# Attention loop of a fused Macaron layer on eight cores: V's projection issued in half pieces, and one more eviction on ScalarE

## The chip, the cores and the metric

The program runs on all 8 cores of one Trainium2 chip. Each core computes one of the 8 sequences of the batch by itself; nothing is exchanged between cores. The metric is the device time of the slowest core in microseconds (us). Everything is in fp32.

## The reference, cut to what matters

```
x = x + 0.5 * ffn(layernorm(x))        # 32 experts x 4 sets, argmax over groups of 32 tokens
x = x + attn(layernorm(x))             # 16 heads of 64, learned relative positions
x = x + 0.5 * ffn(layernorm(x))

def attn(x):                           # x: [2048, 1024] for one core
    Q, K, V = x @ Wq.T + bq, x @ Wk.T + bk, x @ Wv.T + bv      # 16 heads x 64
    scores = (Q K^T + Q . rel_table[clip(i - j + 1023, 0, 2046)]) / 8
    out = softmax(scores) V
    return out @ Wo.T + bo
```

## The kernel before

The kernel is one straight program for each engine, written out by Python loops. An engine runs its own instructions in the order in which they were written; a wait is on a semaphore that another engine raises. What `do(...)` returns is such a token, and `wt(engine, token, ...)` makes the engine wait for it before its next instruction.

**Stages.** The first feed-forward part, then its combine, which also computes the layer norm, transposes it into `HBASE` and projects Q, K and V for the first pair of heads; then the attention loop; then the second feed-forward part with its combine. The change touches the attention loop and the part of the first combine that issues projections.

**The attention loop** (in `emit_attn`) goes over 8 pairs of heads `p`, and for each pair over 16 blocks `q` of 128 query rows: 128 blocks `n = 16 p + q`. A block has four quarters `c` = 0 to 3. In a quarter TensorE gets, in this order:

1. `emit_t(.., 0)`: half of the transposes of 512 columns of the block before (first half, 8 small transposes). They are written to the PSUM banks at `BK_T`, of which there is one set, so they wait for `t_free`, the eviction of the quarter before.
2. `emit_content`: Q K^T for 512 keys (banks `BK_C`).
3. `emit_qr`: Q times the position table for block `n + 2` (banks `BK_Q`), for as many chunks as the block has, 3 or 4. It waits for `qr_free`, the ScalarE eviction of the chunk before.
4. in quarter 2 `emit_rz`, a small transpose.
5. `emit_t(.., 1)`: the second half of the transposes; then `evict_t` copies all 1024 columns to SBUF. Which engine does so depends on the group `g` of transposes: VectorE for `g` 0 and 3, ScalarE for 1 and 2. Group `g` is evicted in quarter `(g + 1) % 4`, so groups 3, 0, 1 and 2 belong to quarters 0, 1, 2 and 3.
6. pieces of the next pair's projections from a `queue` (below).
7. `emit_pv`: probabilities times V for the group of the quarter before.

VectorE adds the two score parts (L888) and takes the maximum (L898) in each quarter. ScalarE evicts the position chunk (L802, L808), and at the end of quarter 3 `emit_softmax` gives it two Exp instructions of 128 x 2048 (L919). In `emit_attn` all this stands in the program ahead of the quarter's pieces.

**The queue of pieces.** `pieces_k`, `pieces_v` and `pieces_q` yield functions. A K or Q projection of 512 tokens is 4 pieces of 2 matmuls, and after the fourth ScalarE evicts it (L689). A V projection of 128 tokens is one piece of 8 matmuls with an eviction on VectorE (L706). All of them share one PSUM bank in the loop, `BK_PJ` (in the combine there are two, `BK_PV` too):

```
pj["banks"] = [BK_PJ]
if part == 0:
    wt("tensor", wtok, pj[bank], h_tok[4 * nb + 2], h_tok[4 * nb + 3])
```

`pj[bank]` is the token of the last eviction from the bank. For pairs 1 to 6 the queue is: the 4 last pieces of Q of this pair, 16 of K, 16 of V, 12 of Q (three quarters of it) of the next pair, 48 in all; for pair 0 it is 44, for pair 7 only 4. Within a pair they are spread over the 64 quarters by this rule:

```
target = max(-(-len(queue) * (4 * q + c + 1) // 64),
             min(len(queue), 4 * q + c + 1, 4))
while done < target:
    queue[done]()
    done += 1
```

In what follows a quarter is written block.quarter, as 13.3 for block 13 of a pair, quarter 3.

Of the kernel before, what the change touches and what calls it, by code (L numbers as in the profile page):

```python
# [15 lines left out]
NPAIR = 8  # L16
NT = 16
# [42 lines left out]
def build_nc():  # L60
# [5 lines left out]
    wvt = nc.dram_tensor("wvt", [DM, DM], F32, kind="ExternalInput").ap()  # L66
# [22 lines left out]
    with ExitStack() as stack:  # L89
# [39 lines left out]
        def ap(off, dims, p0=0, np_=128):  # L129
            return AP(SCR[:, :].tensor, p0 * SCRW + off, [[SCRW, np_]] + dims)  # L130
# [6 lines left out]
        def wt(eng, *toks):  # L137
            for t in toks:
                if t is not None:
                    b.wait(eng, t[0], t[1])  # L140
# [3 lines left out]
        def do(eng, fn, sig=True):  # L144
            if not sig:
                b.op(eng, fn)
                return None
            return (SEM[eng], b.op(eng, fn, inc=SEM[eng]))

        def dma(eng, out, in_, sem):  # L150
            return (sem, b.dma(eng, out, in_, sem))

        def mm(out, lhsT, rhs, start, stop, sig=False, tr=False):
            if tr:
                return do("tensor", lambda e: e.matmul(  # L155
                    out, lhsT, rhs, start=start, stop=stop,
                    is_transpose=True), sig)
            return do("tensor", lambda e: e.matmul(  # L158
                out, lhsT, rhs, start=start, stop=stop), sig)
# [470 lines left out]
        def emit_attn(ffn, in_hbm, src_hbm):  # L630
# [3 lines left out]
            WQ, WK, WV = 6144, 46208, 47232  # L634
# [17 lines left out]
            def load_w(src, off, p, sem):  # L652
                return dma("sync", ap(off, [[128, 8], [1, 128]]),
                           AP(src.tensor, 128 * p,
                              [[DM, 128], [128 * DM, 8], [1, 128]]), sem)
# [11 lines left out]
            h_tok = {}  # L667

            pj = {"banks": [BK_PJ, BK_PV], "i": 0, BK_PJ: None, BK_PV: None}
            state = {"q": [None] * 4, "k": [None, None],  # L670
                     "v": [None, None], "wk": w_k, "wv": w_v, "wq": w_q}
# [19 lines left out]
                    AF.Identity, bias=scr(bof + p, bof + p + 1), scale=scale))  # L691
                return tok

            def proj_v_piece(p, c):
                pj["i"] += 1
                bank = pj["banks"][pj["i"] % len(pj["banks"])]
                wt("tensor", state["wv"] if c == 0 else None, pj[bank],
                   h_tok[c])
                tok = None
                for m in range(8):  # L700
                    tok = mm(PS[:, bank:bank + 128],
                             ap(HBASE + 2048 * m + 128 * c, [[1, 128]]),
                             ap(WV + 128 * m, [[1, 128]]),
                             m == 0, m == 7, sig=(m == 7))
                wt("vector", tok)
                pj[bank] = state["pj"] = do("vector", lambda e: e.tensor_tensor(  # L706
                    ap(VT[p % 2] + 128 * c, [[1, 128]]),
                    PS[:, bank:bank + 128],
                    ap(BVR + 128 * p, [[1, 128]]), ALU.add))
                return tok  # L710

            def pieces_k(p):
                for nb in range(4):
                    for part in range(4):
                        def piece(nb=nb, part=part):
                            tok = proj_qk_piece(p, KT[p % 2], WK, BK, 1.0,
                                                state["wk"], nb, part)
                            if tok:
                                state["k"][p % 2] = state["pj"]
                            if tok and nb == 3 and p + 1 < NPAIR:  # L720
                                wt("sync", tok)
                                state["wk"] = load_w(wkt, WK, p + 1, "wka")
                        yield piece

            def pieces_v(p):
                for c in range(NT):
                    def piece(c=c):
                        tok = proj_v_piece(p, c)
                        state["v"][p % 2] = state["pj"]
                        if c == NT - 1 and p + 1 < NPAIR:  # L730
                            wt("sync", tok)
                            state["wv"] = load_w(wvt, WV, p + 1, "wva")
                    yield piece

            def pieces_q(p, nbs):
                for nb in nbs:
                    for part in range(4):
                        def piece(nb=nb, part=part):
                            tok = proj_qk_piece(p, QT, WQ, BQS, 0.125, state["wq"],
                                                nb, part)  # L740
                            if tok:
                                state["q"][nb] = state["pj"]
                            if tok and nb == 3 and p + 1 < NPAIR:
                                wt("sync", tok)
                                state["wq"] = load_w(wqt, WQ, p + 1, "wqa")
                        yield piece
# [225 lines left out]
            def evict_t(n, g):  # L972
                tok = t_done[n]
                slot = g % 2
                eng = "vector" if g in (0, 3) else "scalar"
                wt(eng, tok, pt_free[slot])
                if eng == "vector":
                    t_free[0] = do("vector", lambda e: e.tensor_copy(  # L978
                        ap(PT[slot], [[1, 1024]]), PS[:, BK_T:BK_T + 1024]))
                else:  # L980
                    t_free[0] = do("scalar", lambda e: e.activation(  # L981
                        ap(PT[slot], [[1, 1024]]), PS[:, BK_T:BK_T + 1024],
                        AF.Copy, scale=1.0))
                pt_tok[(n, g)] = t_free[0]
# [3 lines left out]
            def emit_pv(n, g):  # L988
# [15 lines left out]
                if g == 3:  # L1004
# [12 lines left out]
                    if q % 4 == 3 and n < LAST:  # L1017
# [11 lines left out]
            todo = []  # L1029
            pk, pq, pv = (list(pieces_k(0)), list(pieces_q(0, range(4))),  # L1030
                          list(pieces_v(0)))

            def emit_h_tr(t):
                k = next_pair()
                wt("tensor", hx_t[t], pair_free[k])
                for m in range(8):
                    tok = mm(PS[:, 1024 * k + 128 * m:1024 * k + 128 * (m + 1)],
                             ap(HX[t % 2] + 128 * m, [[1, 128]]),
                             IDENT[:, :], True, True, sig=(m == 7), tr=True)
                tr_t[t] = tok  # L1040
                wt("scalar", tok)
                h_tok[t] = do("scalar", lambda e: e.activation(
                    ap(HBASE + 128 * t, [[2048, 8], [1, 128]]),
                    PS[:, 1024 * k:1024 * (k + 1)], AF.Copy, scale=1.0))
                pair_free[k] = h_tok[t]
                if t % 4 == 3:
                    nb = t // 4
                    todo.extend(pk[4 * nb:4 * nb + 4] + pq[4 * nb:4 * nb + 4]
                                + pv[4 * nb:4 * nb + 4])
                if t == 3:  # L1050
                    todo.extend(lambda n=n, ci=ci: emit_qr(n, ci, True)()
                                for n in (0, 1) for ci in range(4))

            def per_tile(t, src, y):
                if t >= 1:
                    emit_h_tr(t - 1)
                hx_t[t] = emit_ln_tile(t, src, HX[t % 2], y,
                                       (tr_t.get(t - 2),))
                for _ in range(4):
                    if todo:  # L1060
                        todo.pop(0)()
                return (hx_t[t],)
# [37 lines left out]
            for n in range(NIT):  # L1100
                p, q = n // 16, n % 16
                if q == 0:
                    queue = []
                    if p > 0:
                        queue += pieces_q(p, (3,))
                    if p + 1 < NPAIR:
                        queue += pieces_k(p + 1)
                        queue += pieces_v(p + 1)
                        queue += pieces_q(p + 1, range(3))
                    done = 0  # L1110
                for c in range(4):
# [10 lines left out]
                    if tr >= 0:  # L1122
                        emit_t(tr // 4, tr % 4, 1)
                        evict_t(tr // 4, tr % 4)
# [18 lines left out]
            emit_t(NIT - 2, 3, 0)  # L1143
            emit_t(NIT - 2, 3, 1)
            evict_t(NIT - 2, 3)
            emit_pv(NIT - 2, 2)
            emit_pv(NIT - 2, 3)
# [90 lines left out]
```

How the kernel before makes its waits and increments, by code:

```python
    def wait(self, eng, semname, val):  # L40
        if val is None or val <= 0:
            return
        s = self.sems[semname]
        self.th[eng].append(lambda e, s=s, v=val: e.wait_ge(s, v))
# [1 line left out]
    def op(self, eng, fn, inc=None, n=1):  # L46
        if inc is None:
            self.th[eng].append(fn)
            return None
        self.cnt[inc] += n
        s = self.sems[inc]
        self.th[eng].append(lambda e, fn=fn, s=s, n=n: fn(e).then_inc(s, n))
        return self.cnt[inc]
```

## Time and profile before

| | |
|---|---|
| median of 3 runs | 3952.4 us (3952.1 to 3977.1) |
| the profiled execution, its own time | 3966.1 us |
| span of its slowest core (core 1) | 3964.1 us |
| spans of the 8 cores | 3927.9 to 3964.1 us |
| mean granted TensorE clock of the cores | 0.938 to 0.946 |
| attention loop in the span | about 685 to 3215 us |

The profile is of one execution; the rows below are of its slowest core. Start times count from the first instruction of the span. TensorE is PE, VectorE is DVE, ScalarE is ACT, and PEld is the weight load beside the matmuls. A matmul in fp32 shows as two instructions, so a piece of 2 matmuls is 4 of them and 8 matmuls are 16.

### The profile page before, as it was taken

How to read it: one execution, taken by the hardware profiler on the slowest of the kernel's cores; microseconds unless marked ns; L12 is line 12 of the kernel's file. 1: busy time of each engine (PE TensorE's matmuls, PEld its weight loads, DVE VectorE, ACT ScalarE, POOL GpSimd, SP SyncE). 2: the span in 40 equal slices, each digit the busy share in tenths (PEclk: the TensorE clock that was granted, in tenths of full speed). 3: DMA queues.
4: the chain of work that ended last, by engine and by line, in shares of the span. 5: the costliest groups of instructions: out<-in, count | busy, mean ns of one | idle time of the engine just before them, and what ended most of it. 6: DMA issues, size and time to landing. Idle time of an engine off the chain costs nothing.

```text
span 3964.1 us, 80834 instructions; the slowest of 8 cores (3927.9 to 3964.1 us)
## 1 busy us (share of the span) xinstructions
PE 3500.4 (88%) x29664; PEld 2215.0 (56%) x29664; DVE 2097.3 (53%) x2703; ACT 1561.0 (39%) x2013; POOL 187.9 (5%) x289
## 2 busy tenths in 40 slices
PE   6988469999999999999999999999987789988842
PEld 4776134565566566566557557556654545567610
DVE  4333223666666666666666666666675733333311
ACT  3222122544554554554454454455454411122200
POOL 0000000000000000000000000000000000000001
PEclk8799687999999999999999999999998989999965
DMA  4557883564565565465466456456468711156697
GB/s 135 170 188 248 308 257 118 180 200 162 171 208 171 165 206 178 158 203 189 157 193 197 150 184 208 156 173 212 153 188 248 222 55 64 59 178 211 222 320 264
DMA packets 248833, 736.25 MB, mean 186 GB/s; under 512 B 16656, under 2 KB 66320, under 8 KB 240272
## 3 DMA queue, kind: packets, MB, share of 16 engines
q1 hardware_dynamic: 178448, 401.82, 30.7%
q0 software_dynamic: 63680, 317.74, 24.3%
q10 hardware_dynamic: 6336, 11.54, 1.3%
q8 instruction: 260, 4.26, 0.5%
q14 instruction: 109, 0.89, 0.1%
HBM read 405.05 MB, written 325.98 MB: 184 GB/s over the span
## 4 chain that ended last, share of the span: by engine, by line
PE 75%; DMA 13%; ACT 4%; issue 4%; DVE 3%; SPq 0%; POOL 0%; ACTq 0%; DVEq 0%; POOLq 0%
PE PS L158 65%; PE PS L155 10%; DMA out<-SCR 3%; DMA SCR<-f2r 3%; ACT SCR L981 3%; DMA xs<-SCR 3%; DMA SCR<-qsl 1%; DMA SCR<-x 1%; ACT SCR L919 1%; DVE SCR L978 1%; DVE SCR L888 1%; DMA qsl<-SCR 1%; DMA SCR<-itb 0%; DMA SCR<-xs 0%; DVE SCR L898 0%
## 5 line engine op out<-in xcount | busy, mean ns | idle before, releaser
L158 PE MATMUL PS<-SCR 128*64 128x128 f32 (+5 forms) x20928 | 3159.3, 393 | 282.9 <-DMA SCR<-itb 100.4
L158 PEld LDWEIGHTS PS<-SCR 128*64 128x64 f32 (+2 forms) x20928 | 1793.0, 167 | 1174.3 <-issue 1121.0
L888 DVE TENSOR_TENSOR SCR<-PS,SCR 128x1024 f32<-128x1024 f32 (+3 forms) x608 | 642.0, 1056 | 765.9 <-PE PS L158 730.8
L155 PEld LDWEIGHTS PS<-IDENT,SCR 64*128 64x128 f32 (+1 forms) x8736 | 456.5, 141 | 551.8 <-issue 528.6
L155 PE MATMUL PS<-IDENT,SCR 64*128 64x64 f32 (+1 forms) x8736 | 557.7, 236 | 159.2 <-ACT SCR L981 47.2
L898 DVE TENSOR_REDUCE SCR<-SCR 128x2 f32<-128x1024 f32 x512 | 622.5, 1216 | 26.7
L919 ACT ACTIVATE SCR<-SCR 128x2048 f32<-128x2048 f32 x256 | 510.7, 1996 | 122.8 <-DVE SCR L912 122.5
L802 ACT ACTIVATE SCR<-PS 128x1024 f32<-128x1024 f32 (+2 forms) x448 | 413.8, 924 | 259.6 <-PE PS L158 244.2
L981 ACT ACTIVATE SCR<-PS 128x1024 f32<-128x1024 f32 x256 | 262.5, 1025 | 363.8 <-PE PS L155 348.9
L978 DVE COPY SCR<-PS 128x1024 f32<-128x1024 f32 x256 | 311.1, 1215 | 24.9 <-PE PS L155 23.1
L943 ACT ACTIVATE SCR<-PS 128x128 f32<-128x128 f32 x128 | 35.6, 278 | 526.9 <-PE PS L155 517.3
L56 POOL DMA_DIRECT2D SCR<-qsl x128 | 90.9, 710 | 2236.6 <-PE PS L155 1005.3
L619 DVE SCALAR_TENSOR_TENSOR SCR<-PS,SCR 128x1024 f32<-128x1024 f32 x32 | 39.2, 1224 | 256.8 <-DMA SCR<-xs 148.7
L473 DVE COPY SCR<-PS 128x1024 f32<-128x1024 f32 x64 | 78.4, 1225 | 158.6 <-PE PS L158 158.6
L170 ACT ACTIVATE SCR<-SCR 128x1024 f32<-128x1024 f32 x32 | 33.8, 1055 | 298.9 <-DVE SCR L419 214.3
L511 DVE TENSOR_SCALAR SCR<-PS,SCR 32x64 f32<-32x64 f32 x128 | 36.8, 287 | 189.3 <-PE PS L158 186.6
L469 ACT ACTIVATE SCR<-PS 128x1024 f32<-128x1024 f32 x64 | 65.5, 1024 | 159.3 <-PE PS L158 159.3
L506 ACT ACTIVATE SCR<-PS,SCR 32x64 f32<-32x64 f32 x128 | 39.2, 306 | 175.0 <-PE PS L158 173.3
L540 ACT ACTIVATE SCR<-PS 128x1024 f32<-128x1024 f32 x64 | 65.7, 1026 | 97.7 <-PE PS L158 94.4
L415 DVE TENSOR_TENSOR SCR<-PS,SCR 128x1024 f32<-128x1024 f32 x16 | 19.6, 1224 | 148.5 <-PE PS L158 148.5
L537 DVE COPY SCR<-PS 128x1024 f32<-128x1024 f32 x64 | 78.3, 1224 | 35.9 <-PE PS L158 27.5
L56 POOL DMA_DIRECT2D itb<-SCR x64 | 46.0, 719 | 980.9 <-ACT SCR L540 887.7
(47 smaller groups left out, 616.6 us busy)
## 6 DMA issues: line engine op xcount, KB each, us to landing
qsl<-SCR SPq DMA_DIRECT2D x320, 512.0 KB, 4.8
itb<-SCR POOLq DMA_DIRECT2D x64, 1024.0 KB, 13.3
SCR<-itb SPq DMA_DIRECT2D x32, 2048.0 KB, 27.0
SCR<-f1p SPq DMA_DIRECT2D x64, 512.0 KB, 9.1
SCR<-f2r SPq DMA_DIRECT2D x64, 512.0 KB, 12.4
SCR<-qsl POOLq DMA_DIRECT2D x16, 2048.0 KB, 10.7
SCR<-qsl POOLq DMA_DIRECT2D x16, 1920.0 KB, 10.3
SCR<-qsl POOLq DMA_DIRECT2D x16, 1792.0 KB, 10.4
```

What stands on the lines that cost most here:

```text
L56: return self.op(eng, lambda e, o=out, i=in_: e.dma_start(out=o, in_=i), inc=inc, n=16)
L155: return do("tensor", lambda e: e.matmul(out, lhsT, rhs, start=start, stop=stop, is_transpose=True), sig)
L158: return do("tensor", lambda e: e.matmul(out, lhsT, rhs, start=start, stop=stop), sig)
L473: d_t[i] = do("vector", lambda e: e.tensor_copy(dst, src))
L537: e.tensor_copy(dst, src))
L540: e.activation(dst, src, AF.Copy, scale=1.0))
L802: ev = do("scalar", lambda e: e.activation(ap(base, [[640, 2], [1, wd]]), pap(bank, [[512, 2], [1, wd]]), AF.Copy, scale=1.0))
L888: e.tensor_tensor(sr(n, a0, [[1, w]]), pap(BK_C + a0 - j0, [[512, 2], [1, w]]), in1, ALU.add))
L898: return do("vector", lambda e: e.reduce_max(ap(MX + 8 * (n % 2) + step, [[4, 2]]), sr(n, j0, [[1, 512]]), axis=AX.X))
L919: p_tok[(n, h)] = do("scalar", lambda e, h=h: e.activation(sr(n, 0, [[1, 2048]], h), sr(n, 0, [[1, 2048]], h), AF.Exp, bias=scr(nm + h, nm ...
L978: t_free[0] = do("vector", lambda e: e.tensor_copy(ap(PT[slot], [[1, 1024]]), PS[:, BK_T:BK_T + 1024]))
L981: t_free[0] = do("scalar", lambda e: e.activation(ap(PT[slot], [[1, 1024]]), PS[:, BK_T:BK_T + 1024], AF.Copy, scale=1.0))
```

## The change

Two edits. V's piece of 8 matmuls is cut into two pieces of 4 (`part` 0 and 1): the first waits for the bank, the second ends with the eviction. The queue of pairs 1 to 6 so has 64 pieces for 64 quarters, that of pair 0 has 60; the combine, which issues the first pair's projections, takes 5 pieces per tile where it took 4. And group 0 of the transposes is evicted by ScalarE where VectorE did it, so that VectorE has group 3 alone.

```
-            def proj_v_piece(p, c):
-                pj["i"] += 1
+            def proj_v_piece(p, c, part):
+                if part == 0:
+                    pj["i"] += 1
                 bank = pj["banks"][pj["i"] % len(pj["banks"])]
-                wt("tensor", state["wv"] if c == 0 else None, pj[bank],
-                   h_tok[c])
+                if part == 0:
+                    wt("tensor", state["wv"] if c == 0 else None, pj[bank],
+                       h_tok[c])
                 tok = None
-                for m in range(8):
+                for m in range(4 * part, 4 * part + 4):
                     tok = mm(PS[:, bank:bank + 128], ...
                              m == 0, m == 7, sig=(m == 7))
+                if part == 0:
+                    return None
                 wt("vector", tok)
...
             def pieces_v(p):
                 for c in range(NT):
-                    def piece(c=c):
-                        tok = proj_v_piece(p, c)
...
+                    for part in range(2):
+                        def piece(c=c, part=part):
+                            tok = proj_v_piece(p, c, part)
...
             def evict_t(n, g):
-                eng = "vector" if g in (0, 3) else "scalar"
+                eng = "vector" if g == 3 else "scalar"
...
                     todo.extend(pk[4 * nb:4 * nb + 4] + pq[4 * nb:4 * nb + 4]
-                                + pv[4 * nb:4 * nb + 4])
+                                + pv[8 * nb:8 * nb + 8])
...
-                for _ in range(4):
+                for _ in range(5):
                     if todo:
                         todo.pop(0)()
```

The longer queue also moves every piece of K and Q. The rule above gives pairs 1 to 6 exactly one piece per quarter now, so the pieces numbered 4, 8, 12, ... of K and Q, those with an eviction, stand in quarter 3 of a block. Below are ScalarE's instructions around the end of block 1 of pair 3. L919 (before) and L925 (changed) are the two Exp of the softmax, L689 is the eviction of a K projection, L802 and L808 (changed: L808 and L814) evict position chunks, L981 (L987) evicts transposes, L943 (L949) is the small one of quarter 2. Before:

```order
L981 ACTIVATE SCR<-PS 128x1024 [waits pe]
L919 ACTIVATE SCR<-SCR 128x2048 [waits ve]
L919 ACTIVATE SCR<-SCR 128x2048
L802 ACTIVATE SCR<-PS 128x2x512 [waits pe,qwa]
L802 ACTIVATE SCR<-PS 128x2x512 [waits pe,qwb]
L689 ACTIVATE SCR<-PS,SCR 128x512 [waits pe]
L943 ACTIVATE SCR<-PS 128x128 [waits pe,ve]
```

Changed:

```order
L987 ACTIVATE SCR<-PS 128x1024 [waits pe]
L925 ACTIVATE SCR<-SCR 128x2048 [waits ve]
L925 ACTIVATE SCR<-SCR 128x2048
L689 ACTIVATE SCR<-PS,SCR 128x512 [waits pe]
L808 ACTIVATE SCR<-PS 128x2x512 [waits pe,qwa]
L987 ACTIVATE SCR<-PS 128x1024 [waits pe]
L808 ACTIVATE SCR<-PS 128x2x512 [waits pe,qwb]
L949 ACTIVATE SCR<-PS 128x128 [waits pe,ve]
```

The eviction of the K projection has moved from quarter 1 of block 2 to right behind the two Exp, ahead of everything that ScalarE does for quarter 0; and group 0's transposes are a new L987 in quarter 1. In the whole program an L689 stood right behind the two Exp 8 times before, once for each pair, in block 0; it does so 52 times now.

TensorE at the same place, from the end of quarter 3 of block 1 to the piece of quarter 0 of block 2 (64x128 is `emit_pv`, 128x64 a half of the transposes, 128x512 content, position chunk or a piece of K). Before:

```order
L158 MATMUL PS<-SCR 64x128 [waits ac,ve]
L158 MATMUL PS<-SCR 64x128 x7
L155 MATMUL PS<-IDENT,SCR 128x64 [waits ac]
L155 MATMUL PS<-IDENT,SCR 128x64 x7
L158 MATMUL PS<-SCR 128x512 [waits ac,ve]
L158 MATMUL PS<-SCR 128x512
L158 MATMUL PS<-SCR 128x512 [waits ac,ld]
L158 MATMUL PS<-SCR 128x512
L155 MATMUL PS<-IDENT,SCR 128x64 [waits ac]
L155 MATMUL PS<-IDENT,SCR 128x64 x7
L158 MATMUL PS<-SCR 128x512 x2
L158 MATMUL PS<-SCR 64x128 [waits ac,ve]
```

Changed:

```order
L158 MATMUL PS<-SCR 128x512 x2
L158 MATMUL PS<-SCR 64x128 [waits ac,ve]
L158 MATMUL PS<-SCR 64x128 x7
L155 MATMUL PS<-IDENT,SCR 128x64 [waits ac]
L155 MATMUL PS<-IDENT,SCR 128x64 x7
L158 MATMUL PS<-SCR 128x512 [waits ac,ve]
L158 MATMUL PS<-SCR 128x512
L158 MATMUL PS<-SCR 128x512 [waits ac,ld]
L158 MATMUL PS<-SCR 128x512
L155 MATMUL PS<-IDENT,SCR 128x64 [waits ac]
L155 MATMUL PS<-IDENT,SCR 128x64 x7
L158 MATMUL PS<-SCR 128x512 [waits wka,ac]
```

Quarter 3 has a piece now (first row), the last of a projection; and the piece of the next quarter 0 is the first of the next projection, with a wait on ScalarE (`ac`) that no piece had there.

## Rows read from the trace of the kernel before

**Rows 1.** The page's first part: busy time, share, instructions of each engine.

```profile
PE 3500.4 (88%) x29664; PEld 2215.0 (56%) x29664; DVE 2097.3 (53%) x2703; ACT 1561.0 (39%) x2013; POOL 187.9 (5%) x289
```

**Rows 2.** Windows, L943 only, one pair: stretch, length, ACT busy, clock, DMA share, GB/s.

```profile
1330.90:1648.80 317.90, 4.43 (x16) 1.00 0.55 181
```

**Rows 3.** Waits of PE, 1012 to 1330 us: sum, times, longest.

```profile
PE PS L155 <- ACT SCR L981: 6.6, 15, 0.6
PE PS L155 <- ACT SCR L919: 0.7, 1, 0.7
```

**Rows 4.** Timeline of PE, quarters 13.3 (no piece) and 14.0: start, length, instructions, idle.

```profile
1574.22 0.46 PE L155 MATMUL PS<-IDENT,SCR 64*128 64x64 f32 x8
...
1575.43 0.41 PE L155 MATMUL PS<-IDENT,SCR 64*128 64x64 f32 x8
1575.77 1.09 PE L158 MATMUL PS<-SCR 128*64 128x128 f32 x16
1577.28 0.46 PE L155 MATMUL PS<-IDENT,SCR 64*128 64x64 f32 x8 [0.41 <-ACT SCR L981]
...
1579.77 3.01 PE L158 MATMUL PS<-SCR 128*128 128x512 f32 x20
1582.71 0.46 PE L155 MATMUL PS<-IDENT,SCR 64*128 64x64 f32 x8
```

**Rows 5.** Timeline of PE, narrow windows: V's piece, then `emit_pv`, then the next transposes.

```profile
1521.08 0.38 PE L158 MATMUL PS<-SCR 128*128 128x128 f32 x1
...
1523.06 0.44 PE L158 MATMUL PS<-SCR 128*64 128x128 f32 x4
...
1524.08 0.28 PE L155 MATMUL PS<-IDENT,SCR 64*128 64x64 f32 x2
```

**Rows 6.** Timeline of ACT, quarters 0.3 (with L689) and 1.0.

```profile
1633.55 1.02 ACT L981 ACTIVATE SCR<-PS 128x1024 f32<-128x1024 f32 x1 [2.49 <-PE PS L155]
1636.25 2.00 ACT L919 ACTIVATE SCR<-SCR 128x2048 f32<-128x2048 f32 x1 [1.67 <-DVE SCR L912]
...
1638.25 1.99 ACT L919 ACTIVATE SCR<-SCR 128x2048 f32<-128x2048 f32 x1
...
1640.23 0.67 ACT L689 ACTIVATE SCR<-PS,SCR 128x512 f32<-128x512 f32 x1
1640.81 1.00 ACT L802 ACTIVATE SCR<-PS 128x1024 f32<-128x1024 f32 x1
```

**Rows 7.** Timeline of PE, the same quarters 0.3, 1.0 and the start of 1.1.

```profile
1631.77 0.46 PE L155 MATMUL PS<-IDENT,SCR 64*128 64x64 f32 x8
...
1636.26 0.46 PE L155 MATMUL PS<-IDENT,SCR 64*128 64x64 f32 x8
...
1638.67 1.09 PE L158 MATMUL PS<-SCR 128*64 128x128 f32 x16
1640.44 0.46 PE L155 MATMUL PS<-IDENT,SCR 64*128 64x64 f32 x8 [0.68 <-ACT SCR L919]
```

**Rows 8.** Timelines of DVE and PE, quarter 9.0 with a piece of V.

```profile
1482.00 1.22 DVE L978 COPY SCR<-PS 128x1024 f32<-128x1024 f32 x1
...
1480.82 3.08 PE L158 MATMUL PS<-SCR 128*128 128x128 f32 x32
1483.82 0.46 PE L155 MATMUL PS<-IDENT,SCR 64*128 64x64 f32 x8
```

**Rows 9.** Timeline of PE: content and position chunk in quarters 10.1 and 11.1.

```profile
1504.79 1.94 PE L158 MATMUL PS<-SCR 64*128 64x512 f32 x8
...
1524.38 2.14 PE L158 MATMUL PS<-SCR 64*128 64x512 f32 x8
```

**Rows 10.** Pair 7: waits of PE, 2925 to 3185 us; windows, after a 5.25 and a 1.92 us idle.

```profile
PE PS L155 <- DVE SCR L978: 41.4, 27, 5.5
...
3049.20:3053.10 3.90, 3.90 (x16) 1.89 (x18) 2.06 (x2) 0.00 (x0) 0.71 (x1) 0.50 0.36 111
3070.00:3075.00 5.00, 4.34 (x46) 2.68 (x42) 4.18 (x7) 1.02 (x1) 0.71 (x1) 1.00 0.87 184
```

More of the change, by code:

```diff
@@ L726, in pieces_v @@
                 for c in range(NT):
-                    def piece(c=c):
-                        tok = proj_v_piece(p, c)
[L729 to L733, printed above, removed]
+                    for part in range(2):
+                        def piece(c=c, part=part):
+                            tok = proj_v_piece(p, c, part)
+                            if tok:
+                                state["v"][p % 2] = state["pj"]
+                            if tok and c == NT - 1 and p + 1 < NPAIR:
+                                wt("sync", tok)
+                                state["wv"] = load_w(wvt, WV, p + 1, "wva")
+                        yield piece
             def pieces_q(p, nbs):
```

## The prediction

> **What bounds the kernel now.** I read the first part of the page, then the attention loop by windows, then one pair of heads as a timeline. TensorE is busy 88% of the span, no other engine more than 53% [rows 1]. In the loop the clock is full and a pair takes 317.9 us, DMA at 0.55 of its capacity [rows 2], so TensorE's instruction stream and the holes in it are the time. All that the profile shows as its idle time in a pair is 16 waits, 7.3 us together [rows 3]. Each stands in a quarter without a piece: after `emit_pv` the next transposes must wait until the last are evicted, and only a piece of projection covers that. In quarter 13.3 it is 1575.77 to 1577.28, 1.51 us from `emit_pv` to the transposes [rows 4], against 1523.06 to 1524.08, 1.03 with a piece ahead of it [rows 5]: a hole of 0.48, start to start. In 1.0, where VectorE evicts, 1638.67 to 1640.44 is 1.77 [rows 7], a hole of 0.74. The releaser printed there, an Exp, had ended before; VectorE's copy is the one that the program waits for.
>
> **What goes away.** For pairs 1 to 6 every quarter has a piece, so 15 x 0.48 + 0.74 = 8.0 us a pair go. TensorE also waits now and then for a position chunk, where quarter 3 is short and ScalarE is late with Exp and eviction: content and chunk take 2.14 in 11.1 against 1.94 in 10.1 [rows 9]. Two more of this kind, in 1.1 and 13.1, go as the quarters ahead of them get a whole piece: 0.5 by estimate. Gain 8.5 us a pair.
>
> **What the split costs.** V's 8 matmuls take 1521.08 to 1523.06, 1.98 us [rows 5]. Half would be 0.99 if all of it scaled. It doesn't: a piece of K with 4 instructions has the same number of columns and takes nearly the same, 1579.77 to 1582.71 less 1.03, 1.91 [rows 4, 5], so with a quarter of the instructions it isn't shorter in proportion, and some time goes at either end, where one shape of matmul follows another. I take 0.1 us at each of the two ends, by estimate, and 1.09 for a half, bounds 0.99 and 1.2. 16 pairs of halves cost 16 x 0.2 = 3.2 us a pair (0 to 7).
>
> **What the thin cover costs.** Next to a half piece VectorE's copy of group 3 can be late. In 9.0 it ends at 1483.22; the transposes after a copy come 0.25 later, as in 1.0, so at 1483.47, while TensorE would be there at 1480.82 + 1.09 + 1.03 = 1482.94 [rows 8]: 0.5 us. Of the other seven quarters 0 with V, three come out 0.05 to 0.1 short, the rest with slack. The chunk waits of 11.1 and 12.1 grow from 0.2 to about 0.45, since two quarters ahead of each shrink by 0.28 in sum. 1.2 us a pair (0.3 to 3).
>
> **ScalarE's new eviction** of group 0 costs it 1.02 us in quarter 1 (L981 in [rows 6]). In pairs 0 to 6 the chunk eviction behind it still ends before the next chunk needs its bank, by about 1 us, and the piece covers both engines' eviction: nothing on the path; were that cover gone, 1 us in each of 112 blocks. In pair 7, which has no pieces beyond block 0, VectorE's copy is what TensorE waits for, 41.4 us in 27 waits, four of them of 5 us behind a position read [rows 10]. 1.22 becomes 1.02 in 14 blocks: 3 us gained (0 to 3).
>
> **What is moved, and this decides.** The pieces of K and Q move too. The last piece of each group of four now always stands in quarter 3, and `emit_softmax` is written ahead of it; so its eviction L689 is queued on ScalarE behind both Exp. The next piece, in quarter 0, is the first of a group and writes the same, only bank: it waits for L689. Behind that piece stand, in TensorE's order, `emit_pv`, the next transposes, everything. The trace has this eviction in this place once a pair, in 0.3, where the quarter after has no piece and it hurts nobody. Quarter 0.3 starts at 1631.77 [rows 7]; the Exp run from 1636.25, 4.48 later, L689 from 1640.23 to 1640.90 [rows 6], that is 9.13 after the quarter's start. With some 0.14 to the release (0.25 for transposes), TensorE goes on at 9.27. What the Exp wait for, content, sum and maximum of the quarter, is the same in each quarter 3, so I use 9.27 for all.
>
> When would TensorE be there? A short quarter 3 with a whole piece is 1631.77 to 1636.26, 4.49 [rows 7]; the piece of quarter 0 comes 1577.28 to 1579.77, 2.49 later [rows 4]: at 6.98. Wait 2.3 us. So in 0.0, 2.0 and 15.0; in 1.0 it is 2.4 (1636.26 + the 2.41 to 1638.67). Quarters 2.3, 3.3, 4.3 have a fourth, narrower chunk, a quarter, half and three quarters of the 0.94 of a full one: waits of 2.1, 1.8 and 1.6 in 3.0, 4.0 and 5.0. In 14.0 it is worse: the position chunk for block 0 of the next pair needs the very Q that L689 of 13.3 evicts, and it is due 1.21 (1574.22 to 1575.43, [rows 4]) plus some 0.06 into the quarter, at 5.76: 3.5 us, and then the piece waits no more. A pair: 3 x 2.3 + 2.4 + 2.1 + 1.8 + 1.6 + 3.5 = 18.3 us.
>
> By the queue's arithmetic pairs 2 to 6 have 8 such places, pair 1 has 7 (its 0.0 follows pair 0, whose last eviction stands in quarter 2), pair 0 has 3 (1.0, 2.0, 3.0), pair 7 one: 51 places. The order of ScalarE bears it out, 52 evictions right behind the Exp, the last without a piece after it.
>
> **The sum.** Pairs 2 to 6: -8.5 + 3.2 + 1.2 + 18.3 = +14.2, times 5 = +71. Pair 1: +12. Pair 0: 20 quarters without a piece become 4, about -9; +3.2 +1.0 +6.8: +2. Pair 7: +2.3 - 3 = -1. The combine issues the same work in other portions, and its order differs by half a V piece at most: 0 (0 to +2), hidden by its LayerNorm chain and, at the end, only moved. Total +84 us on the profiled execution's 3966.1 (2.1%). That one lay 13.7 above the median; I put the same 84 on the median, 3952.4: **4036 us**.
>
> What the other way of counting would say: all waits go, nothing comes back. The Trainium skill ("Perfetto Trace Analysis", Matmuls under Optimizing Tensor Performance) says that independent matmul groups should rotate through different PSUM banks, so that an eviction overlaps the next group. This loop has a single bank for its pieces, so by that rule the piece after an eviction is exposed; here that has been hidden, since three pieces in four quarters left L689 in quarters 0 to 2, ahead of no Exp. By the rule alone I could not size it; the size is that of rows 6 and 7.
>
> **Rivals.**
> - *Only the holes close.* If L689 did not hold TensorE (because the piece waits for something earlier, or ScalarE gets to it between the Exp), the 117 us of such waits (3 + 7 + 40 + 1 places) fall out: 4036 - 117 = 3919 us. For it: 16 holes a pair are real [rows 3] and each does get a piece. Against: the order shows the wait on ScalarE at the first piece of a group, and the row of 0.3 shows L689 after the second Exp. Chance 0.06, the other side.
> - *The clock falls in the longest wait.* After an idle 5.25 us the granted clock was 0.50, the lower of its two levels (1.2 GHz), for the whole stretch 3049.2 to 3053.1; after 1.92 us it was 1.00 [rows 10]. The 3.5 us of 14.0 lie between. With a fall the content and chunk behind it take 3.9 instead of 2.2: +1.7 x 6 = 10 us, 4046. The Trainium skill ("TensorE: Matmul & The Clock Gate", HAM oscillation) says that idle gaps between matmuls return the clock to its low level; the 5.25 us row agrees. Chance 0.2.
> - *Most, not all, of the waits.* If the Exp start earlier or the quarters stretch so that a wait is 1.5 us on average, not 2.3, the cost is 77 and not 117: 3996. Nothing in the rows makes VectorE's chain (content, add, maximum) shorter, so 0.07.
> - *The cover fails in V's blocks.* They shrink from about 19.8 to 17.5 us, and the position reads have that much less time; blocks of pair 7 ran at 17.15 us before the output weights were loaded, without a wait for a read. Were one of 8 such blocks a pair late by 5 us, +30: 4066. Chance 0.04.
>
> **How the numbers follow.** The forecast, with all three terms as above, has 0.6; the rivals take 0.37 and leave 0.03 for something unseen. A measurement of this kernel tells about 1%, 40 us, from no change. Slower by over 1%: the forecast, the clock, the reads and nearly all of the third rival, 0.90. The first rival, at -0.8%, lies by its bounds half within 1% and half beyond: faster 0.03; within 1% 0.07, with the rest. The terms' bounds around 4036: split -20 to +25, thin cover -6 to +12, and 10 either way if each of 51 waits is 0.2 us off. The range, 4000 to 4062, takes these in, the clock, and the upper half of the third rival.
>
> **What would show it.** In the changed profile: no PE wait on L981 in pairs 1 to 6; a new one, PE L158 on ACT L689, about 45 times 2 us; L689 right behind the second Exp; half a V piece at 1.09; quarter 13.3 at 4.49 and 14.0 near 9; a pair at 332 us where it was 318; V's blocks near 17.5. I am wrong if L689 starts before the Exp are through, or if the first piece of a group doesn't wait.

## The result: slower by 2.6%, and the profile after

The changed kernel takes 1.0259 times the time of before, 95% interval 1.0209 to 1.0309; on the 3952.4 us of before that is 4055 us, +102 (83 to 122). The forecast was 4036 us, +84, in a range from 4000 to 4062. Of the five executions of the changed kernel two, 4057.5 and 4062.2 us, had all cores at their usual clock, and the ratios here compare such executions alone. The profiled execution took 4057.5 us.

The page's first part, against [rows 1]: VectorE has 128 evictions less, ScalarE 128 more, and of the 92 us by which the span has grown TensorE was busy in 15 and idle in 77.

```profile
PE 3514.9 (87%) x29664; PEld 2200.2 (54%) x29664; DVE 1962.3 (48%) x2575; ACT 1675.4 (41%) x2141; POOL 187.8 (5%) x289
```

One pair by windows, as in [rows 2] (length, ScalarE busy, clock, DMA share, GB/s):

```profile
1644.50:1982.40 337.90, 4.42 (x17) 0.98 0.51 171
```

The pair takes 337.9 us where it took 317.9, and its mean clock is 0.98 where it was 1.00 [rows 2]. The waits of TensorE in the same pair, against [rows 3]:

```profile
PE PS L158 <- ACT SCR L689: 19.9, 8, 3.6
PE PS L155 <- ACT SCR L808: 0.5, 1, 0.5
PE PS L155 <- DVE SCR L984: 0.4, 1, 0.4
```

The 16 small waits for an eviction of transposes are gone, and eight for L689, the eviction of a K or Q projection, have come. The L808 named in the second row had ended before; in both small rows TensorE waited for VectorE's copy (L984), the one that the program waits for there. The timelines of TensorE and ScalarE in quarters 1.3 and 2.0 of the pair, the place that stands in the order ahead of the prediction:

```profile
1671.18 0.46 PE L155 MATMUL PS<-IDENT,SCR 64*128 64x64 f32 x8
...
1672.73 3.01 PE L158 MATMUL PS<-SCR 128*128 128x512 f32 x20
1675.67 0.46 PE L155 MATMUL PS<-IDENT,SCR 64*128 64x64 f32 x8
...
1680.67 2.98 PE L158 MATMUL PS<-SCR 128*128 128x512 f32 x20 [2.52 <-ACT SCR L689]
...
1675.66 2.00 ACT L925 ACTIVATE SCR<-SCR 128x2048 f32<-128x2048 f32 x1 [1.68 <-DVE SCR L918]
...
1677.66 1.99 ACT L925 ACTIVATE SCR<-SCR 128x2048 f32<-128x2048 f32 x1
...
1679.65 0.67 ACT L689 ACTIVATE SCR<-PS,SCR 128x512 f32<-128x512 f32 x1
```

Quarter 3 begins at 1671.18 and the Exp start 4.48 us later, as read from [rows 6, 7]; L689 ends 9.14 after the quarter's start (9.13 forecast), and TensorE resumes at 9.49 (9.27 forecast). In blocks 4 and 14 the piece after the wait also takes longer, 1727.68 to 1732.23 less 1.03 is 3.5 us, where it takes 1.9. Timeline and windows of these places; in the windows the granted clock is the number behind the busy times of the five engines:

```profile
1727.68 4.62 PE L158 MATMUL PS<-SCR 128*128 128x512 f32 x20 [2.10 <-ACT SCR L689]
1732.23 0.46 PE L155 MATMUL PS<-IDENT,SCR 64*128 64x64 f32 x8
...
1921.18 1.18 PE L158 MATMUL PS<-SCR 64*128 64x512 f32 x4 [3.62 <-ACT SCR L689]
...
1922.72 4.40 PE L158 MATMUL PS<-SCR 128*128 128x512 f32 x20
...
1727.60:1731.00 3.40, 3.32 (x4) 1.18 (x4) 1.01 (x1) 0.63 (x1) 0.71 (x1) 0.50 0.55 116
1922.10:1925.50 3.40, 3.40 (x14) 1.65 (x10) 2.35 (x2) 1.02 (x1) 0.70 (x1) 0.51 0.34 78
1731.50:1734.00 2.50, 2.50 (x32) 1.61 (x30) 0.20 (x1) 0.00 (x0) 0.00 (x0) 1.00 0.97 387
```

The granted clock was 0.50 for 3.4 us, its lower level of 1.2 GHz, and back at 1.00 after. In pairs 1 to 6 there were 16 to 18 such stretches on each core, some of them twice as long; before there was none on any.

Where the time lies, as the mean of the eight cores of each profiled execution, measured from the small eviction (L943, L949) of one block 0 to that of the next. The two executions differ by 93 us in this mean, where the ratio above gives 102:

| stretch | before | after | difference |
|---|---|---|---|
| pair 0 (from its block 1) | 298.4 | 292.2 | -6.2 |
| pairs 1 to 6, sum | 1908.2 | 2028.4 | +120.2 |
| pair 7 | 294.8 | 288.6 | -6.2 |
| all of the loop | 2501.5 | 2609.1 | +107.6 |
| up to the loop | 679.2 | 665.0 | -14.2 |
| after the loop | 766.2 | 765.8 | -0.4 |

The stage up to the loop varies from run to run: two experiments below with its code of before had 670.0 and 663.9 there. So I don't credit the change with its 14 us. Part of the differences ahead of pair 1 comes from the profile of before: on its cores 0 to 3 the granted clock was 0.81 for 48 us ahead of the loop and for 34 to 54 us at its start, and they took 299.6 to 302.3 us in the row of pair 0. Its cores 4 to 7, at 1.00 in the loop, took 295.6 us there, the changed kernel 291.7 to 292.0 on seven of its cores. Between cores at full clock the row of pair 0 is -3.8 and not -6.2.

### The profile page after: what moved, and what is told of

Its sections match the earlier page's. It is cut to its first block, busy times and chain, and to the rows that moved or that the text cites. A ratio compares the mean times of both kernels' runs of the same rounds, so it can differ in the third digit from the quotient of the medians.

```text
span 4056.0 us, 80834 instructions; the slowest of 8 cores (4012.2 to 4056.0 us)
## 1 busy us (share of the span) xinstructions
PE 3514.9 (87%) x29664; PEld 2200.2 (54%) x29664; DVE 1962.3 (48%) x2575; ACT 1675.4 (41%) x2141; POOL 187.8 (5%) x289
## 4 chain that ended last, share of the span: by engine, by line
PE 69%; DMA 13%; issue 7%; DVE 5%; ACT 5%; SPq 0%; POOL 0%; DVEq 0%; ACTq 0%; POOLq 0%
PE PS L158 61%; PE PS L155 9%; DMA out<-SCR 3%; DMA SCR<-f2r 3%; ACT SCR L925 3%; DMA xs<-SCR 2%; DVE SCR L894 2%; DVE SCR L904 2%; DMA SCR<-qsl 1%; DMA qsl<-SCR 1%; DMA SCR<-x 1%; ACT SCR L689 1%; DMA SCR<-itb 1%; ACT SCR L987 1%; ACT SCR L808 0%
## 5 line engine op out<-in xcount | busy, mean ns | idle before, releaser
L158 PE MATMUL PS<-SCR 128*64 128x128 f32 (+4 forms) x20928 | 3183.0, 393 | 407.8 <-ACT SCR L689 139.5
L155 PEld LDWEIGHTS PS<-IDENT,SCR 64*128 64x128 f32 (+1 forms) x8736 | 447.0, 140 | 504.8 <-issue 482.3
L987 ACT ACTIVATE SCR<-PS 128x1024 f32<-128x1024 f32 x384 | 392.9, 1023 | 766.5 <-PE PS L155 751.5
L925 ACT ACTIVATE SCR<-SCR 128x2048 f32<-128x2048 f32 x256 | 510.6, 1996 | 121.9 <-DVE SCR L918 121.5
L808 ACT ACTIVATE SCR<-PS 128x1024 f32<-128x1024 f32 (+2 forms) x448 | 413.5, 923 | 31.5 <-PE PS L158 25.5
L949 ACT ACTIVATE SCR<-PS 128x128 f32<-128x128 f32 x128 | 35.5, 277 | 361.3 <-PE PS L155 361.3
L984 DVE COPY SCR<-PS 128x1024 f32<-128x1024 f32 x128 | 155.6, 1216 | 38.8 <-PE PS L155 38.5
L473 DVE COPY SCR<-PS 128x1024 f32<-128x1024 f32 x64 | 78.4, 1225 | 160.2 <-PE PS L158 160.2
L170 ACT ACTIVATE SCR<-SCR 128x1024 f32<-128x1024 f32 x32 | 33.8, 1055 | 295.6 <-DVE SCR L419 213.9
L469 ACT ACTIVATE SCR<-PS 128x1024 f32<-128x1024 f32 x64 | 65.5, 1023 | 160.8 <-PE PS L158 160.8
L540 ACT ACTIVATE SCR<-PS 128x1024 f32<-128x1024 f32 x64 | 65.6, 1025 | 102.5 <-PE PS L158 90.0
L537 DVE COPY SCR<-PS 128x1024 f32<-128x1024 f32 x64 | 78.4, 1224 | 40.9 <-PE PS L158 28.2
```

The source lines that it names most:

```text
L155: return do("tensor", lambda e: e.matmul(out, lhsT, rhs, start=start, stop=stop, is_transpose=True), sig)
L158: return do("tensor", lambda e: e.matmul(out, lhsT, rhs, start=start, stop=stop), sig)
L473: d_t[i] = do("vector", lambda e: e.tensor_copy(dst, src))
L537: e.tensor_copy(dst, src))
L540: e.activation(dst, src, AF.Copy, scale=1.0))
L808: ev = do("scalar", lambda e: e.activation(ap(base, [[640, 2], [1, wd]]), pap(bank, [[512, 2], [1, wd]]), AF.Copy, scale=1.0))
```

## The experiments

### 1. The piece ahead of the Exp

```
                     evict_qr()
...
-                    if c == 3:
-                        emit_softmax(n, mx)
...
                     while done < target:
                         queue[done]()
                         done += 1
+                    if c == 3:
+                        emit_softmax(n, mx)
```

> The changed kernel, but in every quarter 3 the queue's piece is written ahead of the softmax, so that ScalarE evicts a finished K or Q projection (L689) before the two Exp and not behind them; TensorE's order is the same. Theory 1 (the loss is TensorE waiting for L689 behind the Exp, and the clock falls that these waits bring): both go, 20.4 + 5 us of a pair of 337.9, to about 312.6 us, below the 318.0 of before; in all about 3906 us, 1.2% faster than before. Rival (the split itself, 64 pieces where 48 were and half the cover in V's blocks, is what costs): nearly nothing comes back, 4040 to 4060 us. Rival 2 (the clock falls have another cause): the waits go, the granted clock still falls three times a pair, about 317 us a pair, 3935 us.

Measured: 0.9833 of before (0.9811 to 0.9856; every ratio here is to the kernel before, run beside the experiment), median 3895.0 us. A pair is 312.5 us, and no core shows a clock fall in pairs 1 to 6. ScalarE's timeline at a projection's end, quarter 3 and the start of the next block, and the window of a pair:

```profile
1652.61 1.02 ACT L987 ACTIVATE SCR<-PS 128x1024 f32<-128x1024 f32 x1 [2.98 <-PE PS L155]
...
1654.46 0.69 ACT L689 ACTIVATE SCR<-PS,SCR 128x512 f32<-128x512 f32 x1
1655.05 1.99 ACT L925 ACTIVATE SCR<-SCR 128x2048 f32<-128x2048 f32 x1
...
1584.20:1896.70 312.50, 4.44 (x16) 1.00 0.58 184
```

L689 goes ahead of the Exp, into time in which ScalarE waited for VectorE anyway. Theory 1 had 312.6 a pair; by the rival, that the split is what costs, nearly nothing would have come back, and by the second rival the clock falls would have stayed. So the whole loss of the change, and more, came from the place of this eviction. The version beats both kernels.

### 2. Probabilities times V ahead of the piece

```
+                    if tr >= 1:
+                        emit_pv((tr - 1) // 4, (tr - 1) % 4)
                     while done < target:
                         queue[done]()
                         done += 1
-                    if tr >= 1:
-                        emit_pv((tr - 1) // 4, (tr - 1) % 4)
```

> The changed kernel, but TensorE gets a quarter's probabilities times V ahead of the quarter's piece; ScalarE's order is the same, L689 stays behind the Exp. Theory 1: TensorE reaches the waiting piece 1.03 us later, so 7 of the 8 waits of a pair are 1.03 us shorter (2.5 becomes 1.5) and the eighth, for the position chunk of 14.0, stays at 3.6 us; 45 x 1.03 = 46 us less than the changed kernel, and if shorter waits bring fewer clock falls up to 20 us more: 3990 to 4014 us. If TensorE were held by something else than L689 (VectorE's copy, a DMA), the order would not matter: 4057 us.

Measured: 1.0164 (1.0129 to 1.0200), 4029 us, above the 3990 to 4014 expected; a pair is 332.0 (mean of pairs 1 to 6 on all cores), with 6 clock falls a core in place of 16 to 18, all in 14.0. The loop is 33 us shorter than the changed kernel's (2576.5 against 2609.1), where 46 to 66 were expected. TensorE's waits in one pair, and a quarter 2:

```profile
PE PS L158 <- ACT SCR L689: 12.7, 8, 3.6
PE PS L158 <- ACT SCR L949: 3.2, 16, 0.5
...
1693.09 0.72 PE L155 MATMUL PS<-IDENT,SCR 128*128 128x128 f32 x9
1694.00 3.01 PE L158 MATMUL PS<-SCR 128*64 128x128 f32 x20 [0.18 <-ACT SCR L949]
```

The waits for L689 shrank as the theory says, from 19.9 to 12.7, 7 x 1.03; the one in block 14 stayed at 3.6, and it is the one that still lets the clock fall. What I had not seen is the second row: in quarter 2 `emit_pv` needs the small eviction of that quarter, which the piece had covered. From the transposes of quarter 2 to what follows them it is 0.91 us here (1693.09 to 1694.00) and 0.65 in the changed kernel (1691.09 to 1691.74), 16 x 0.26 = 4 us a pair. 338.0 - 7.2, less 2 falls of 1.6 to 1.7, + 4.2 is 331.7.

### 3. L689 on VectorE

```
-                wt("scalar", tok)
-                pj[bank] = state["pj"] = do("scalar", ... activation Identity, bias, scale)
+                wt("vector", tok)
+                pj[bank] = state["pj"] = do("vector", ... tensor_scalar, bias (and scale))
```

> The changed kernel, but K's and Q's projections are evicted by VectorE (add of the bias, or multiply and add) and no more by ScalarE. Theory 1: what hurts is ScalarE's queue. VectorE is through with the quarter's maximum 5 us into quarter 3, so the bank is free before TensorE comes 7 us into it: the waits and the falls go as in the run with the piece ahead of the Exp, 3905 to 3920 us. Rival (the bank is simply single, and any eviction in quarter 3 is too late for quarter 0): waits stay, over 4000 us.

Measured: 0.9875 (0.9832 to 0.9919), 3917 us, 312.5 to 313.1 us a pair, no clock falls. With one bank and with the eviction still in quarter 3 the waits for it are gone here too. So neither the single bank nor the late quarter makes the loss by itself; the queue behind two Exp has to come with them.

### 4 and 5. The second edit taken back, and alone

In the changed kernel, and the opposite edit in the kernel before:

```
-                eng = "vector" if g == 3 else "scalar"
+                eng = "vector" if g in (0, 3) else "scalar"
```

> The changed kernel, but group 0 of the transposes is evicted by VectorE again, as before; only V's split is left of the change. Theory 1: this eviction is no cause of the loss; pair 7 is 3 us slower by the longer copy on its path, elsewhere 0 to 1 us a pair where VectorE is tight in V's short blocks: 0 to 10 us over the changed kernel, 4057 to 4067 us. Rival (ScalarE is late because of the eviction it was given): L689's waits shrink and the time falls by over 20 us.

Measured: 1.0292 (1.0246 to 1.0337), within the interval of the changed kernel; the executions compared took 4061 to 4092 us, 4057 to 4067 were expected. Pairs 2 to 4 are 337.7 to 338.0 us, the waits for L689 in one pair 20.0 us in 8, as with the edit. Pair 7 is 296.3 us, against 288.6. On cores 0 and 1 pairs 5 and 6 took 343 to 350 us: the granted clock was 0.81 there for 162 us, from 2601 us on. Core 4 had one pair of 341 us, with the clock at 0.50 for longer than in the others.

> The kernel before with the second edit alone: group 0 of the transposes evicted by ScalarE. Theory: no effect in pairs 0 to 6 (318.0 a pair, the piece covers either eviction); in pair 7 the copy on TensorE's path is 0.2 us shorter in 14 blocks: 3949 us, 3 less than before, not measurable; its pair 7 shows it.

Measured: 0.9961 (0.9914 to 1.0008): not to be told from before, as expected. Pair 7 is 290.6 us (mean of cores), against 294.8; the other pairs 318.0 to 318.4. The edit is harmless, and worth some 4 us in the pair without pieces.

### 6 and 7. Controls for the repair

The reordering of experiment 1 in the kernel before:

> The kernel before, with the one edit that repaired the changed one: in quarter 3 the piece is written ahead of the softmax. L689 stands behind the Exp in one block of a pair only, and the quarter after that has no piece. Theory 1: nothing is to be gained here, 3945 to 3956 us, a pair 317.5 to 318.0; the 1.7% of the repaired kernel is due to the fuller queue. Rival (the order of Exp and piece is worth something by itself): under 3930 us.

Measured: 0.9988 (0.9954 to 1.0023), a pair 317.7 us. The order alone is worth nothing; the 1.7% come from it together with the fuller queue.

The repaired kernel with group 0 on VectorE:

> The repaired kernel (piece ahead of the softmax), but group 0 on VectorE again: what the second edit is worth once the waits are gone. Theory: V's short blocks leave VectorE some 0.5 us of slack a quarter, so 312.5 to 314 us a pair; pair 7 3 us longer; 3898 to 3907 us. Rival (the second edit is needed for V's short blocks, VectorE becomes late for the sum of the next quarter): 316 us a pair and more, over 3915 us.

Measured: 0.9856 (0.9802 to 0.9911), a pair 312.6 to 313.0, pair 7 293.8 us against 288.4. V's short blocks don't need the second edit; the rival had 316 a pair.

### 8. The waits filled

```
+            def fill(k):
+                for i in range(k):
+                    mm(pap(BK_PV, [[1, 128]], 0, 64), IDENT[0:64, 64:128],
+                       ap(GT, [[1, 128]], 0, 64), False, False)
...
+                    if c == 0 and q == 14 and p + 1 < NPAIR:
+                        fill(15)
...
+                    if c == 0 and (n in (2, 3) or
+                                   (1 <= p < 7 and q in (1, 2, 3, 4, 5, 15))
+                                   or (p >= 2 and q == 0)):
+                        fill({3: 9, 4: 8, 5: 6}.get(q, 10))
```

> The changed kernel with the waits for L689 left as they are and filled: in 50 of the 51 quarters 0 concerned TensorE gets 6 to 15 matmuls of 64x64 weights that are all zero, with 128 columns, into the open sum of probabilities times V, ahead of the piece that waits (in block 14 ahead of the position chunk). They add zero, so nothing else is changed, and are to take somewhat less than the wait. Theory 1 (three of the eight waits of a pair let the granted clock fall, at 1.6 us each): no falls in the loop, a pair 333 us where it was 338, about 4027 us. Rival (the clock has nothing to do with these waits, or its fall costs nothing): 338 us a pair, 4057 us. If the filler takes longer than the wait, a pair is over 338.

Measured: 1.0169 (1.0125 to 1.0213), 4033 to 4038 us. This interval just touches that of the changed kernel (1.0209 to 1.0309), so the reading rests on the pairs and not on the total. Window of one pair and TensorE's timeline in quarters 1.3 and 2.0:

```profile
1631.90:1964.90 333.00, 4.49 (x17) 1.00 0.54 173
...
1658.52 0.46 PE L155 MATMUL PS<-IDENT,SCR 64*128 64x64 f32 x8
...
1665.42 2.39 PE L158 MATMUL PS<-SCR,IDENT 64*64 64x128 f32 x20
1668.01 2.98 PE L158 MATMUL PS<-SCR 128*128 128x512 f32 x20 [0.20 <-issue]
```

The piece starts 9.49 us after quarter 3's start, to the hundredth where it started without the filler, so the piece is held as long as before; the clock is 1.00 throughout, with no falls on any core in pairs 1 to 6, and a pair is 333.0. The clock falls cost 5.0 us a pair, 30 in pairs 1 to 6: three a pair at 1.6 to 1.7 us. The total is above the 4027 expected. 3.5 us of that come from the edit itself, which also fills block 14 of pair 0, where the changed kernel has no wait (pair 0 took 295.7 us against 292.2).

## Why the prediction was right, and its sizes

**The mechanism** was the one forecast: 51 first pieces in quarter 0 behind an eviction behind two Exp, eight in a pair. Experiments 1 and 3 remove the queueing in two ways and both take the whole loss away; 2 shortens the waits by what was worked out, 7 x 1.03 a pair. That TensorE waits for the bank, and not for the copy of the transposes, is shown by 2, where only the place of the piece moved.

**The wait** was forecast as 18.3 us a pair and measured 20.5, start to start (19.9 of idle time, and some 0.07 at each place between the idle time and the start that TensorE would have had, 0.17 in 14.0): 9.49 and not 9.27 us after quarter 3's start. L689 ended when it was said to (9.14); the release to a piece of K took 0.35 us, where I had taken 0.14 from an `emit_pv` behind ScalarE. This term was some 0.2 us too small at each place, 10 in the loop.

**The clock** was a rival at 0.2, with a fall in 14.0 alone. It fell in 14.0 each time and, on the mean, at two more of the eight places, mostly 0.0 and 4.0; that is 5.0 us a pair by experiment 8, where the forecast had nothing and the rival 1.7. This is the larger part of the miss. The step that failed was to bracket the fall between an idle of 1.92 and one of 5.25 us and then to take all waits of 2.5 us or less as harmless, without a row that shows it.

**The gain** was a little larger than 8.5 us a pair. A pair would be 318.0 - 8.5 + 3.2 + 1.2 = 313.9 without the waits, and 312.5 was measured in the repaired kernel. After a hole the quarter itself is slower: quarter 14.0 took 1577.28 to 1582.71, 5.43 us [rows 4]; the same instructions without a hole ahead take 5.35 (quarter 2.1 of the changed kernel, 1683.58 to 1688.93). I counted the hole alone; 16 x 0.08 to 0.09 are 1.3 to 1.4.

**The split** costs what was taken: half a piece of V and `emit_pv` in the changed kernel, 1812.30 to 1814.41, is 2.11, less 1.02 for `emit_pv` is 1.09.

```profile
1812.30 2.18 PE L158 MATMUL PS<-SCR 128*128 128x128 f32 x24
1814.41 0.46 PE L155 MATMUL PS<-IDENT,SCR 64*128 64x64 f32 x8
```

**The thin cover** costs about 1.7 us a pair (1.2 forecast): by start times holes of 0.56 and 0.49 us in 9.0 and 11.0, 0.48 at the chunk of 12.1, and some 0.6 in smaller ones, less 0.4 that the kernel before had at its chunks in 11.1 and 12.1. In 9.0, where the sum has two parts, VectorE's copy ends at 1828.06 and the transposes come at 1828.31; TensorE would have been there at 1827.75, a hole of 0.56, as forecast from [rows 8] (0.5):

```profile
1826.84 1.22 DVE L984 COPY SCR<-PS 128x1024 f32<-128x1024 f32 x1
...
1825.64 2.18 PE L158 MATMUL PS<-SCR 128*128 128x128 f32 x24
1828.31 0.46 PE L155 MATMUL PS<-IDENT,SCR 64*128 64x64 f32 x8 [0.49 <-ACT SCR L808]
```

**ScalarE's new eviction** was forecast at nothing in pairs 0 to 6 and 3 us gained in pair 7. By experiments 5 and 7 it is within 1 us in the sum of pairs 1 to 6; in pair 7 it gained 4 to 8 us by experiments 4, 5 and 7.

**Pair 0** was forecast at +2, with 2.4 of it for the wait in 1.0. The stretch of the table begins behind that wait, so its forecast is -0.4; between cores at full clock it has -3.8. That is 3.4 us more gain than forecast, and no run shows from what. The wait in 1.0 itself was 4.3 us long.

Together for a pair: +14.2 forecast; 2.2 more wait, 5.0 of clock, 0.5 more thin cover, 1.4 less by the holes' second part: +20.5, against +20.0 measured; the 0.5 left over isn't traced. The range held the time because the bounds of its terms are wide; of the clock it took in 10 us, and 30 came. Some luck was in it too. Pairs 1 to 6, with the wait in 7.0, were forecast at +85 and came out at +120, while pair 0, pair 7 and the stage ahead of the loop together came out some 25 us below their forecast, 14 of which are the stage that also varies without the change.

**The rivals.** That only the holes close is what the repaired kernel does, 3895 us; I had 3919 for it. The terms without the waits give a loop 33 us shorter, and by the two profiles it is 50.5 us shorter (2451.0 against 2501.5). That a position read would be late in V's blocks did not happen: in pairs 1 to 6 no core of the changed kernel shows a long wait of TensorE but those for L689, though the blocks with V's pieces ran at 17.7 to 18.8 us.

## What to carry to other kernels

When work is spread over slots by a table or a rule, look where the instructions go that a piece issues on other engines, above all the one that frees its buffer: here a regular filling put it, each time, behind the longest instructions of that engine's queue, where an irregular one had missed them by chance. Here the added pieces paid only where their own eviction was queued ahead of the work that would delay it; writing the piece a few lines earlier made 2.6% slower into 1.7% faster. And count a repeated wait on TensorE at more than its length, as long as a run hasn't shown that the clock survives it.

## What was not expected of the hardware

The clock fell in waits shorter than the profile of before let me think. Idle 1.92 us it had stayed at 1.00 and after 5.25 it was 0.50 [rows 10]; in the changed kernel it was 0.50 around an idle of 2.10 us (block 4 above), while at the same pair's 2.52 us in block 2 the piece behind the wait ran at full speed. So the length of one idle doesn't decide it; what does, these runs don't settle. Over the eight cores and pairs 1 to 6 the clock fell at all 48 idles of 3.6 us in 14.0, at 26 of the 48 of 2.1 to 2.3 us in 4.0 and at none of the 48 of 1.8 us in 5.0; of the idles of 2.5 us it was 43 of the 48 in 0.0 (pairs 2 to 7) and 1 of the 48 in 15.0. The same kernel has its falls at other blocks on other cores. And the filler's matmuls, whose weights are all zero, kept the clock at 1.00 (experiment 8). Whether fewer or smaller ones would, no run shows.
